# LayerNorm statistics in PSUM and a residual addition in four pieces, in a gated graph convolution

## The reference

```python
h = jnp.maximum(_layernorm(x, axis=-1), 0.0)
z = jnp.concatenate([h[src], h[dst], edge_attrs], axis=-1)
m = jax.nn.sigmoid(z @ W_f + b_f) * jax.nn.softplus(z @ W_s + b_s)
message = jax.ops.segment_sum(m, src, num_segments=100000)
mean = jnp.mean(message, axis=0)
var = jnp.mean((message - mean) ** 2, axis=0)
out = x + h + (message - mean) * jax.lax.rsqrt(var + 1e-5) * gamma + beta
```

## Time and profile before

| | us |
|---|---|
| median of 3 runs | 1170.78 (1169.67 to 1173.92) |
| profiled execution | 1171.02 |
| its span, first to last instruction | 1169.3 |

### The profile page before, as it was taken

One profiled execution on the slowest core, in us unless ns is written; L12 is line 12 of the kernel. 1 busy time (PEld: TensorE's weight loads), 2 busy tenths in 40 slices (PEclk: granted clock), 3 DMA queues, 4 the chain that ended last, 5 costly groups with the idle time before them and its releaser, 6 DMA issues. The chain is left out here.

```text
span 1169.3 us, 12404 instructions
## 1 busy us (share of the span) xinstructions
PE 789.8 (68%) x3499; PEld 593.6 (51%) x3499; DVE 692.2 (59%) x1176; ACT 483.4 (41%) x1119; POOL 731.1 (63%) x596
## 2 busy tenths in 40 slices
PE   0678866766685776867676686676667126689976
PEld 0457755555563655656464565556456125533322
DVE  1357665655647565564746556475668315679956
ACT  0356645545354454535445453544547014400000
POOL 5747787887878788787888878788785630000000
PEclk9866757566656656556666655756667559989979
DMA  7966443434344332332323233232323259859998
GB/s 276 388 248 204 99 78 80 84 72 99 58 99 79 77 80 41 63 44 60 61 43 61 41 63 46 56 61 42 62 38 63 13 154 401 334 160 398 428 426 362
DMA packets 78283, 161.99 MB, mean 139 GB/s; under 512 B 39759, under 2 KB 46255, under 8 KB 69679
## 3 DMA queue, kind: packets, MB, share of 16 engines
q1 hardware_dynamic: 22575, 80.90, 19.1%
q0 software_dynamic: 40768, 19.31, 16.0%
q10 hardware_dynamic: 14912, 61.46, 13.4%
HBM read 93.87 MB, written 67.75 MB: 138 GB/s over the span
## 5 line engine op out<-in xcount | busy, mean ns | idle before, releaser
L328 POOL DMA_INDIRECT xg<-in_x_dram,gidx x392 | 381.4, 973 | 139.9 <-issue 114.6
L340 POOL DMA_INDIRECT msgs_dram<-comb,target x196 | 348.6, 1779 | 78.9 <-issue 57.3
L409 DVE TENSOR_REDUCE row_sum<-xg 128x24 f32<-128x1536 f32 (+2 forms) x53 | 86.4, 1630 | 315.6 <-DMA xg<-in_x_dram,gidx 311.1
L551 ACT ACTIVATE sq<-xc 128x1536 f32<-128x1536 f32 (+2 forms) x53 | 73.3, 1384 | 283.9 <-DVE xc L417 254.8
L686 PE MATMUL ps_z<-ident,xc 128*128 128x128 f32 x196 | 52.4, 420 | 172.1 <-DVE xc L466 172.1
L712 PE MATMUL ps_c<-msg,same 128*128 128x64 f32 x980 | 160.4, 337 | 9.8 <-issue 5.3
L712 PEld LDWEIGHTS ps_c<-msg,same 128*128 128x128 f32 x980 | 159.5, 256 | 10.2 <-issue 5.5
L699 PEld LDWEIGHTS ps_v<-w_e,ea_t 128*128 128x128 f32 x392 | 101.9, 319 | 71.0 <-issue 71.0
L699 PE MATMUL ps_v<-w_e,ea_t 128*128 128x128 f32 x392 | 128.5, 430 | 0.0
L686 PEld LDWEIGHTS ps_z<-ident,xc 128*128 128x128 f32 x196 | 34.4, 211 | 182.0 <-DVE xc L466 182.0
L696 PE MATMUL ps_v<-b_row,ones 1*128 1x512 f32 x98 | 96.5, 1084 | 40.7 <-ACT z_t L574 37.7
(11 more groups left out here) (93 smaller groups left out, 978.3 us busy)
## 6 DMA issues: line engine op xcount, KB each, us to landing
m_buf<-msgs_dram SPq DMA_DIRECT2D x38, 1024.0 KB, 20.7
msgs_dram<-zeros ACTq DMA_DIRECT2D x16, 1536.0 KB
xg<-in_x_dram SPq DMA_DIRECT2D x48, 512.0 KB
out_dram<-m_buf ACTq DMA_DIRECT2D x20, 1024.0 KB, 10.9
y_spill_dram<-y_kept ACTq DMA_DIRECT2D x19, 512.0 KB
y_kept<-y_spill_dram SPq DMA_DIRECT2D x9, 1024.0 KB, 30.4
xg<-in_x_dram,gidx POOLq DMA_INDIRECT x392
msgs_dram<-comb,target POOLq DMA_INDIRECT x196
```

The source lines that it names most:

```text
L328: pool.indirect_dma_start(xg[:, slot, 2 * j + c, :], None, x, bass.IndirectOffsetOnAxis(ap=gidx[:, g.slot(UNROLL), c, j:j + 1], axis=0),). ...
L340: pool.indirect_dma_start(msgs, bass.IndirectOffsetOnAxis(ap=target[:, g.slot(UNROLL), j:j + 1], axis=0), comb[:, g.slot(UNROLL), j, :], N ...
```

## The change

`row_sum` and `row_rstd` go from SBUF to PSUM, a bank for each. To free a bank, `ps_e` is placed in the bank of `ps_c`. TensorE then turns z first and the edges after it, and waits before the edges for ScalarE's copy of `ps_c` of the same step; ScalarE makes this copy ahead of the squares, no longer behind the gates. The residual addition is issued as four additions of four rows (256 elements per partition) each. VectorE does the target computation ahead of it, and the four pieces alternate with the four counting operations, a count first.

```diff
-        row_sum = sb("row_sum", [P, ROWS])
-        row_rstd = sb("row_rstd", [P, ROWS])
-        ps_e = ps("ps_e", [P, P])
-        ps_c = ps("ps_c", [P, TILES, F])
+        bank_c = ps("bank_c", [P, TILES * F + P])
+        ps_c = bank_c[:, 0:TILES * F].rearrange("p (t f) -> p t f", f=F)
+        ps_e = bank_c[:, TILES * F:TILES * F + P]
+        row_sum = ps("row_sum", [P, ROWS])
+        row_rstd = ps("row_rstd", [P, ROWS])
...
-            def count_not_later(g):
-                wait_group(dve, src_spread, g)
-                wait_group(dve, later_done, g.back(1))
-                for b in range(TILES):
-                    ins = dve.scalar_tensor_tensor(
+            def count_not_later(g, b):
+                if b == 0:
+                    wait_group(dve, src_spread, g)
+                    wait_group(dve, later_done, g.back(1))
+                ins = dve.scalar_tensor_tensor(
...
-                dve.tensor_tensor(y_kept[:, bass.ds(row, BULK), :], xc[:, g.slot(2), GATHERED:ROWS, :],
-                                  xg[:, g.slot(SLOTS), GATHERED:ROWS, :], ALU.add).then_inc(y_done, 1)
+                n = BULK // TILES
+                row = (g.n - SKEW) * BULK - (0 if spill else SPILL * BULK) + part * n
+                rows = slice(GATHERED + part * n, GATHERED + (part + 1) * n)
+                ins = dve.tensor_tensor(y_kept[:, bass.ds(row, n), :], xc[:, g.slot(2), rows, :],
+                                        xg[:, g.slot(SLOTS), rows, :], ALU.add)
+                if part == TILES - 1:
+                    ins.then_inc(y_done, 1)
...
                     normalise(g.back(1))
-                    residual(g.back(1), spill)
                 if g.back(3).exists():
                     targets(g.back(3))
+                for part in range(TILES):
+                    if g.back(2).exists():
+                        count_not_later(g.back(2), part)
+                    if in_steps(g.back(1)):
+                        residual(g.back(1), spill, part)
                 if g.back(2).exists():
-                    count_not_later(g.back(2))
                     softplus(g.back(2))
...
                     softplus_log(g.back(2))
+                if g.back(3).exists():
+                    copy_comb(g.back(3))
                 if in_steps(g):
                     square(g)
...
                     gates(g.back(2))
-                if g.back(3).exists():
-                    copy_comb(g.back(3))
...
                 wait_group(pe, ea_copied, g.back(1))
+                wait_group(pe, comb_copied, g.back(2))
...
                 if g.back(1).exists():
+                    turn_z(g.back(1))
                     turn_edges(g.back(1))
-                    turn_z(g.back(1))
```

More of the change, by code:

```diff
@@ L427, in sum_squares @@
                 dve.tensor_reduce(row_ssq[:, rows], sq[:, rows, :], AX.X, ALU.add).then_inc(ssq_done, 1)
-            def count_not_later(g):
-                wait_group(dve, src_spread, g)
-                wait_group(dve, later_done, g.back(1))
-                for b in range(TILES):
-                    ins = dve.scalar_tensor_tensor(
-                        out=not_later[:, b, :], in0=ps_src[:, b, :], scalar=own[:, g.slot(UNROLL), b:b + 1],
-                        in1=upto[:, :], op0=ALU.is_equal, op1=ALU.mult, accum_out=no_later[:, b:b + 1])
-                ins.then_inc(not_later_done, 1)
+            def count_not_later(g, b):
[3 more added lines that the diff above has]
+                ins = dve.scalar_tensor_tensor(
+                    out=not_later[:, b, :], in0=ps_src[:, b, :], scalar=own[:, g.slot(UNROLL), b:b + 1],
+                    in1=upto[:, :], op0=ALU.is_equal, op1=ALU.mult, accum_out=no_later[:, b:b + 1])
+                if b == TILES - 1:
+                    ins.then_inc(not_later_done, 1)
             def targets(g):
@@ L469, in normalise, with residual @@
                                          op0=ALU.max, op1=ALU.mult).then_inc(h_done, 1)
-            def residual(g, spill):
+            def residual(g, spill, part):
                 if not g.nodes():
-                    dve.sem_inc(y_done, 1)
+                    if part == TILES - 1:
+                        dve.sem_inc(y_done, 1)
                     return
[L475 to L478, removed]
-                dve.tensor_tensor(y_kept[:, bass.ds(row, BULK), :], xc[:, g.slot(2), GATHERED:ROWS, :],
-                                  xg[:, g.slot(SLOTS), GATHERED:ROWS, :], ALU.add).then_inc(y_done, 1)
+                if part == 0:
+                    wait_group(dve, h_done, g)
+                    if not spill:
+                        dve.wait_ge(spilled, 16 * SPILL)
+                n = BULK // TILES
[3 more added lines that the diff above has]
+                                        xg[:, g.slot(SLOTS), rows, :], ALU.add)
+                if part == TILES - 1:
+                    ins.then_inc(y_done, 1)
             def message(g):
@@ L571, in copy_turned @@
                 wait_group(act, v_done, g.back(1))
-                act.activation(ea_t[:, :], ps_e[:, :], ACT.Copy).then_inc(ea_copied, 1)
+                act.activation(ea_t[:, :], ps_e, ACT.Copy).then_inc(ea_copied, 1)
                 wait_group(act, z_turned, g)
@@ L603, in copy_comb @@
                 wait_group(act, slots_free, g)
-                act.activation(comb[:, g.slot(UNROLL), :, :], ps_c[:, :, :], ACT.Copy).then_inc(comb_copied, 1)
+                act.activation(comb[:, g.slot(UNROLL), :, :], ps_c, ACT.Copy).then_inc(comb_copied, 1)
             def spill(g):
@@ L669, in turn_edges @@
                 wait_group(pe, ea_copied, g.back(1))
-                pe.transpose(ps_e[:, :], eas[:, g.slot(SLOTS), :, :].rearrange("p t f -> p (t f)"),
+                wait_group(pe, comb_copied, g.back(2))
+                pe.transpose(ps_e, eas[:, g.slot(SLOTS), :, :].rearrange("p t f -> p (t f)"),
                              ident[:, :]).then_inc(ea_turned, 1)
```

## The result

The changed kernel takes 1249.09 us (median of 4, 1247.68 to 1250.31) where the kernel before took 1172.35 on the same chip: 1.066 times as long, 95% interval 1.063 to 1.068. The forecast was 1133 us. The profiled execution took 1248.32 us, its span is 1246.3, 77 us more than before.

A forecast was written before the change was run, and what follows sets the result against it. GpSimd's own issue was taken to bound the kernel. Saving 0.87 us a group gave -34 us over 39 groups, stage ends -4 and -3.5, start-up +3: 1171.0 - 38.5 = 1132.5, said as 1133 us, range 1123 to 1152.

The forecast's parts named there:

- What bounded the kernel: Edge groups: GpSimd's own issue sets the 18.54 us period, so only shortening a GpSimd instruction pays.
- the centring's hold: VectorE's centring, reading two SBUF tensors, lengthens a GpSimd scatter; row_sum in PSUM was to save 0.95 us a group.
- the second rival: The long scatter isn't the centring's, so nothing is gained and start-up costs 3 us: 1174 us; chance 0.04.
- The normalisation with one input in PSUM holds nothing: With row_rstd in PSUM, VectorE's normalisation was to cost the fourth scatter 0, where two SBUF inputs would cost 0.65 us a group.
- The first rival: The normalisation still holds GpSimd up with one input in PSUM, 0.65 us a group, 26 us: 1159 us; chance 0.08.
- The pieces: Four residual additions between counts were to hold two gathers by 0.16 us a group, bounds 0 to 0.62; VectorE's extra 0.5 hidden.
- TensorE's loop: TensorE's chain with z, comb copy and edges was to take 16.7 us against a 17.67 us period, costing nothing in steady state.
- The third rival: ScalarE's comb copy and squares enter TensorE's loop, making it 18.9 us a group: 1188 us; chance 0.04.
- The start-up: Before 96 us the chain isn't hidden: +3 us, between 0 and +6; from 96 to 135 us, -4.0.

The follow-up runs named there:

- x2: Changed kernel with row_sum and row_rstd both back in SBUF; 1176.88 us beside 1172.83 for the kernel before, on chip D.
- x4: Changed kernel with row_sum alone back in SBUF; 1.001 of the kernel before, on chip D.
- x5: Changed kernel with the residual whole at its old place, ahead of the counts; 1146.38 us beside 1171.42 for the kernel before, on chip E.
- e7: e4 with the residual whole at its old place; 0.974 of the kernel before on chip B, 0.975 on chip E.
- e4: Kernel before with both statistics in PSUM, four pieces, z turned first, ps_e sharing row_sum's bank; 0.964 of before on chip A, 1.044 on C, 1.033 on E.
- e5: Changed kernel with ScalarE's comb copy moved behind the squares; 1223.82 us, 1.043 of the kernel before, on chip B.
- e6: Changed kernel with the comb copy released by the last combining product, ahead of the column sums; 1214.59 us, 1.035 of the kernel before, on chip B.
- e8: Changed kernel with the edges turned ahead of z; 1240.68 us, 1.057 of the kernel before, on chip B.
- e1: Kernel before with ps_e in ps_c's bank and the changed TensorE and ScalarE order, statistics in SBUF, residual whole; 1.001 of before on chip A, 1.005 on C.

## Why the prediction was wrong

**What bounded the kernel, and the centring's hold: right.** The scatters fell to 1569 ns, against "near 1570"; gathers stayed at 962, under the 970 named. That a long scatter isn't the centring's (the second rival) is excluded: it comes back with `row_sum` in SBUF (x2, x4) and goes with it in PSUM. By the Trainium skill, SBUF — State Buffer, "Who interferes with whom", a two-input operation shouldn't stall a DMA's descriptors, which the page itself calls inferred; these runs disagree by 0.84 us in the earlier trace rows and 1.05 in the row at 107.84.

**The normalisation with one input in PSUM holds nothing: right.** The first rival is out: mean scatter 1569 to 1572 ns in x5 and e7. Where `row_rstd` stays in SBUF a hold appears, 0.70 and 0.76 us a group (1744 and 1759 ns) where 0.65 was worked out.

**The pieces: the price in view was right, the term was wrong.** They hold gathers for little: in e4 the mean gather is 975 ns on chip A and 962 on chip E, in e7 with the whole residual 996 on chip E. The step gave the pieces 0.16 us a group for GpSimd and took VectorE's extra time out of idle time. It asked only what they do to GpSimd. They cost 2.0 us a group in e4 against e7 on chip E (19.6 less 17.6; 69 us in all), and the changed kernel lies 2.6 above x5 (20.4 less 17.8, not run side by side), both with TensorE's later release.

**TensorE's loop: this is the step that failed.** "16.7 us against a new period of 17.67; it stays hidden with 1 us of margin" rests on the earlier trace rows, which ends the sums at their shown end, 520.90. ScalarE's copy there is no witness, as it waits in its queue for other work. The increment is at 521.43. That is only 0.53 us later, but it is half of the margin. In groups where the granted clock was 1.0 it is 4.2 us behind the shown end, at the same 15.0 us after the bias product. So "where the clock is higher there is more" was wrong as well: the shown ends move with the granted clock, the release didn't. With 15.0 us and the 2.6 us from the release to the next product that the circle takes, it is 17.6 us, against 17.67 no margin at all. The larger error is that TensorE's part was taken as fixed: in the changed kernel the release comes at 18.0 us in the median and 17.9 in the mean, and with 2.6 that is the period that was measured, near 20.4. Why it moved by 3 us is the open point above, and nothing in the rows before the change told of it.

**The third rival named the mechanism in part**, with too small a chance (0.04) and price. `comb` copy and squares did enter the loop, priced at 18.9 us a group; it came to 20.4. But they are the smaller part. On chip C e4, whose circle holds neither, has 20.0 us a group against the changed kernel's 21.4, where GpSimd's own work needs 17.7 (e4 on chip A). e5 and e6, which take the squares or the sums out, gain 0.5 and 0.7 us a group against e8 on the same chip. And the counter-argument, that normalised rows come at 522.0 and so TensorE waits for them anyway, held only as long as GpSimd led: in the closed circle the normalisation ends (516.42) ten us before it is needed.

**The start-up was mis-sized too.** It was put at +3 us, with gains of 4 to set against it, and so the eighth products at 134.7. They start at 159.4 in the changed kernel, through the same circle.

**Where the circle is open, the sum was near.** x5: period 17.82 against 17.67, which is 6 us; its eighth products start at 142.0, where they started at 135.7 before and 134.7 was forecast, 7 us; the rest agrees to 1 us. Together 1146.4 against 1132.5. e4 on chip A took 1124.15. Of the kernels that ran, e7 was the fastest off chip A (1142.43 and 1141.79 us on chips E and B); x5, on chip E alone, is 0.3% behind it.

## What to carry to other kernels

Before an engine that sets the pace is made faster, list every circle of waits beside it and take its length from what a waiting engine shows (the start of its next instruction, or the semaphore), never from the shown ends of matmuls: here they were up to 9 us early. Two edits of which none does harm alone can close such a circle together (the pieces 0.999 on chip A, the rest of the change 0.978 on chip E, both 1.066, and 1.097 on chip C), so they are to be measured together and apart, and on more than one chip where the margin is a microsecond. A pipeline in which two circles are nearly equal may stay in the slower one for good, once the start-up has put it there. The changed kernel stayed there for 40 groups and e7 left it within ten; that the start-up alone decides is not shown.

## What was not expected of the hardware

TensorE's increment behind the sums comes 4 to 9 us after their shown end, by the median of each kernel, in all traces but those of chip A (8.1 us in the row at 526.45). It comes 0.5 us after it in those groups of the kernel before where the record has 0.5. On chip A it comes within 0.02 us of it in all four kernels, with the same instructions. The kernel before is almost as fast on all chips (1166.43 to 1175.89 us), as e1 is (1.001 and 1.005) with releases of 10.4 and 15.5 us; the kernel with the other bank layout and pieces goes from 0.964 to 1.044. And the mean granted clock in the records is no measure of it: the stretch after has 0.67 and the later release, the one before 0.60 and the earlier one.
